# Cross attention of layer 1: context turned between the two key halves of a chunk, and transfers of weights and key pairs issued in other stages' programs

## Chip, core and metric

One core of a Trainium2 chip runs one program in one launch. Its engines are TensorE (PE), VectorE (DVE), ScalarE (ACT), GpSimd (POOL) and SyncE (SP); SP only issues transfers. The metric is the device time of that program in microseconds (us), lower is better.

## What is computed

Two layers act on `x`, 2 batches of 256 tokens by 256, with a context of 2 by 4096 rows of 192 numbers. Each layer is a cross attention into the context, a mixing stage and an expert mixture. The change concerns layer 1's cross attention and the borders to its neighbours:

```python
x = x + cross(layernorm(x), ctx)          # layer 1, 16 heads of 16
# in cross:
Qp = query @ Wq + bq
K = l2norm(ctx @ Wk + bk)                 # norm over all 256 columns of a row
V = ctx @ Wv + bv
Q = l2norm(Qp)
attn = softmax(Q @ K.T * SCALE)           # per head, 256 queries x 4096 keys
out = (attn @ V) @ Wo + bo + Qp
return layernorm(out) * gamma + beta
```

Before it stands layer 0's expert mixture, behind it layer 1's self attention (weights `w_q, w_k, w_v, w_o`), then layer 1's expert mixture.

## The kernel before

The program is a chain of blocks (`nc.Block()`). In a block each engine has its own instruction list, ordered by semaphores; at its end all five engines meet, so **a block lasts as long as its longest list**, SP's list of transfer issues too. A transfer's issue takes an engine's time, while its bytes travel on their own; a block does not wait for bytes unless an instruction in it does.

`l1_cross_attention` runs these blocks in order:

1. `l1x_weights`: `start_loads` issues 14 transfers, half on SP and half on ACT (line 1258); `finish_loads` is a block in which SP waits for all of them; then ACT and DVE split Wk and Wv into a high and a low part, `s.wkv` (L2181, L2188).
2. `l1x_queries`: layernorm of `x` (L131 to L158), the product with Wq, query norms, turned queries.
3. For each batch `l1x_keys_values`: 8 chunks of 512 context rows. A chunk's rows are turned by PE into PSUM banks 0 and 1 (`turn`, L541); ACT copies them to `cA_hi` and `cB` (L2313, L2314) and DVE makes the low parts (L2353, L2355). PE projects the two key halves d = 0 and 1 into banks 2 and 3 (L2265); ACT keeps their high part (L2320, two instructions for a half) and DVE the low part (L2364), ACT squares them (L2326), POOL adds the squares, PE sums them (L2283), DVE keeps the sums (L2380). PE projects values into banks 4 and 5 (L2275) and DVE keeps these (L2372). Chunk c+1 is turned while chunk c is projected. Chunks 2 to 5 are in a hardware loop on PE and DVE, 0 to 5 on ACT; the rest is written out.
4. For each batch `l1x_attention`: 128 steps of scores (L2470), exponential (ACT, L2455) and weighting (L2482). Keys come from `k_pairs`, a buffer of two halves. A half (16 steps) is filled by 12 transfers out of `keys` (`load_key_pairs`, L2418). There are 8 fillings for a batch; fillings 0 and 1 are issued at the end of `l1x_keys_values`, when the keys of chunks 0 to 3 and of 4 to 7 are there, and the others in the attention, each when its half has been used.
5. `fetch_l1_self_attention` (6 transfers) and `fetch_l1_mixture` (6 transfers) are blocks that only issue; then comes `l1x_output`: output product, bias, layernorm, sum into `x`.

The order in a chunk before is written out by hand:

```python
# PE:  project_keys(c) (both halves); turn(c + 1); sum_squares(c - 1); project_values(c)
# ACT: keys_hi(c, 0); keys_hi(c, 1); context_hi(c + 1); squares(c, 0); squares(c, 1)
# DVE: keys_lo(c, 0); keys_lo(c, 1); context_lo(c + 1); keep_norms(c - 1); keep_values(c)
```

Of the kernel before, what the change touches and what calls it, by code (L numbers as in the profile page):

```python
# [22 lines left out]
P = 128  # L23
# [1734 lines left out]
def l0_mixture(core, s):  # L1758
# [4 lines left out]
    with ExitStack() as ctx:  # L1763
# [11 lines left out]
        with ExitStack() as late:  # L1775
# [13 lines left out]
            with nc.Block() as block:  # L1789
                @block.tensor  # L1790
# [93 lines left out]
def fetch_l1_mixture(core, ctx):  # L1884

    s = Tiles()
    s.w_gu = core.sbuf(ctx, "w_gate_up1", [P, 2, 2, DC, M1])
    s.wd = core.sbuf(ctx, "w_down1", [P, 2, MT, D])
    s.arrived = [core.sem(ctx, f"moe1_w_arrived{i}", lasting=True) for i in range(2)]
    routed, _ = routed_weights(core)  # L1890
    with core.nc.Block() as block:
        @block.sync
        def _(sp):
            for e in range(2):
                fetch_expert(s, sp, e, routed, e)
    return s
# [178 lines left out]
def l1x_queries(core, s):  # L2075
# [3 lines left out]
    with ExitStack() as ctx:  # L2079
        xnT = core.sbuf(ctx, "xnT_l1x", [P, DC, T])  # L2080
        wq, bq = s.wq, s.bq
# [17 lines left out]
        with nc.Block() as block:  # L2099
            @block.tensor  # L2100
# [56 lines left out]
def l1x_weights(core, s):  # L2157

    nc, a = core.nc, core.args
    with ExitStack() as ctx:  # L2160
        raw = core.sbuf(ctx, "wkv1_raw", [P, 2, 2, D])
        hi = core.sem(ctx, "wkv1_hi")
        pairs = []
        for i, n in enumerate("kv"):
            w = a[f"L1_xattn_W{n}"]
            pairs += [(raw[:, 0, i, :], w[0:P, :]), (raw[0:CB, 1, i, :], w[P:CD, :]), (raw[CB:P, 1, i, :], w[P:CD, :])]
        finish_loads(core, start_loads(core, ctx, pairs + [
            (s.wq[:, :, :], a["L1_xattn_Wq"].rearrange("(c p) n -> p c n", p=P)),
            (s.bq[:, :], broadcast_rows(a["L1_xattn_bq"], P)),
            (s.bk[:, :], columns(a["L1_xattn_bk"])),  # L2170
            (s.bv[:, :], broadcast_rows(a["L1_xattn_bv"], P)),
            (s.bo[:, :], broadcast_rows(a["L1_xattn_bo"], P)),
            (s.gamma[:, :], broadcast_rows(a["L1_xattn_ln_gamma"], P)),
            (s.beta[:, :], broadcast_rows(a["L1_xattn_ln_beta"], P)),
            (s.wo[:, :, :], a["L1_xattn_Wo"].rearrange("(c p) n -> p c n", p=P)),
        ], "l1w"))
        with nc.Block() as block:
            @block.scalar
            def _(act):
                for c in range(2):  # L2180
# [11 lines left out]
def l1x_keys_values(core, b, s, keys, values, inv_norm, k_ready):  # L2192
# [5 lines left out]
    with ExitStack() as ctx:  # L2198
# [22 lines left out]
        with nc.Block() as block:  # L2221
# [12 lines left out]
            def _(sp):  # L2234
# [6 lines left out]
                for half in range(2):  # L2241
                    if b == 0:
                        sp.wait_ge(pairs_padded, half + 1)
                    sp.wait_ge(k_hi, (half + 1) * CHUNKS * 2)
                    sp.wait_ge(k_lo, (half + 1) * CHUNKS * 2 + 4)
                    load_key_pairs(sp, s, keys, 0, half, k_ready)

            @block.tensor
            def _(pe):
# [8 lines left out]
                def project_keys(c, slot):  # L2258
                    pe.wait_ge(c_hi, c * 2 + 4)
                    pe.wait_ge(c_lo, c * 2 + 4)  # L2260
                    for d in range(2):
                        pe.wait_ge(k_lo, c * 4 + 2 * d + 2)
                        pe.wait_ge(squared, c * 2 + d + 1)
                        for n, (part, operand) in enumerate(passes):
                            last = pe.matmul(psum[:, 2 + d, :], s.wkv[:, part, d * P:(d + 1) * P], operand[:, slot, :],  # L2265
                                             start=n == 0, stop=n == len(passes) - 1)
                        last.then_inc(k_done, 1)
# [701 lines left out]
```

## Time and profile before

| | us |
|---|---|
| median of 3 runs | 2123.61 |
| lowest, highest | 2123.42, 2126.72 |
| the profiled execution | 2128.06 |
| its span, first to last instruction | 2126.4 |
| mean granted TensorE clock | 0.942 of full |

The profiled execution lies 4.45 us above the median of the runs, and its span 1.66 us below its own time. Times in the rows are us from the span's start. In a timeline row stand the start, the busy time of the merged instructions, the engine (SPq and ACTq are their transfer issues, PEq is PE's sequencer), the line, the output and inputs with their sizes, the count, and in brackets the idle time of that engine just before with what ended it.

### The profile page before, as it was taken

How to read it: one execution, taken by the hardware profiler on the slowest of the kernel's cores; microseconds unless marked ns; L12 is line 12 of the kernel's file. 1: busy time of each engine (PE TensorE's matmuls, PEld its weight loads, DVE VectorE, ACT ScalarE, POOL GpSimd, SP SyncE). 2: the span in 40 equal slices, each digit the busy share in tenths (PEclk: the TensorE clock that was granted, in tenths of full speed). 3: DMA queues.
4: the chain of work that ended last, by engine and by line, in shares of the span. 5: the costliest groups of instructions: out<-in, count | busy, mean ns of one | idle time of the engine just before them, and what ended most of it. 6: DMA issues, size and time to landing. Idle time of an engine off the chain costs nothing. (4 is left out here: it accounts for less than half of the span.)

```text
span 2126.4 us, 33376 instructions
## 1 busy us (share of the span) xinstructions
PE 1898.8 (89%) x13464; PEld 1274.8 (60%) x13464; DVE 1096.3 (52%) x1550; ACT 1029.4 (48%) x1363; POOL 649.9 (31%) x315
## 2 busy tenths in 40 slices
PE   6899999999899999999999666948898899666999
PEld 2576766666566676766666344438444744343887
DVE  2577676675766758676550444238001700273665
ACT  1254454444544445444441322026897699524443
POOL 1026564554545646555473030011000100010000
PEclk9899999999999999999999786969999999877999
DMA  5410000001200000000030100023553446300221
GB/s 189 134 43 6 6 16 1 16 6 42 59 1 16 6 16 6 6 11 6 1 79 1 59 1 1 0 63 84 85 91 70 92 68 103 98 1 2 90 90 40
DMA packets 89923, 90.59 MB, mean 43 GB/s; under 512 B 29928, under 2 KB 79824, under 8 KB 86448
## 3 DMA queue, kind: packets, MB, share of 16 engines
q1 hardware_dynamic: 86912, 86.01, 16.7%
q10 hardware_dynamic: 2864, 2.51, 0.4%
q8 instruction: 107, 1.75, 0.4%
q14 instruction: 40, 0.33, 0.0%
HBM read 58.57 MB, written 8.91 MB: 32 GB/s over the span
## 5 line engine op out<-in xcount | busy, mean ns | idle before, releaser
L760 POOL TENSOR_TENSOR sums<-sums,probs 128x1024 f32<-128x1024 f32 x224 | 534.6, 2386 | 355.0 <-ACT probs L793 305.2
L844 DVE TENSOR_REDUCE part_max<-psum_banks 128x2 f32<-128x1024 f32 (+1 forms) x256 | 312.7, 1224 | 125.8 <-PE psum_banks L1006 121.3
L793 ACT ACTIVATE probs<-psum_banks 128x1024 f32<-128x1024 f32 x240 | 245.8, 1024 | 123.3 <-PE psum_banks L1052 116.1
L1066 PE MATMUL psum_banks<-probs,values 128*64 128x256 f32 x2048 | 278.4, 393 | 0.3 <-ACT probs L796 0.3
L771 ACT ACTIVATE keys<-psum_banks 64x512 fp32r<-64x512 f32 x256 | 151.6, 592 | 239.7 <-PE psum_banks L979 236.6
L2455 ACT ACTIVATE probs<-psum_banks,k_inv_norm 128x1024 f32<-128x1024 f32 x256 | 258.0, 1257 | 2.2 <-PE psum_banks L2470 2.2
L837 DVE TENSOR_TENSOR keys<-psum_banks,keys 64x512 fp32r<-64x512 f32 x256 | 176.2, 688 | 117.8 <-ACT keys L771 111.6
L1034 PE MATMUL psum_banks<-q_hi,keys 128*128 128x256 f32 x1024 | 184.6, 302 | 0.0
L1066 PEld LDWEIGHTS psum_banks<-probs,values 128*64 128x64 f32 x2048 | 124.4, 136 | 99.8 <-issue 60.1
L1034 PEld LDWEIGHTS psum_banks<-q_hi,keys 128*128 128x128 f32 x1024 | 138.0, 189 | 76.7 <-issue 51.7
L776 ACT ACTIVATE values<-psum_banks 128x512 f32<-128x512 f32 x128 | 76.5, 598 | 192.8 <-PE psum_banks L991 192.8
L2482 PE MATMUL psum_banks<-probs,values 128*32 128x256 f32 x2048 | 166.1, 397 | 2.3 <-ACT probs L2455 2.3
L2470 PEld LDWEIGHTS psum_banks<-q_parts_turned,k_pairs 64*128 64x128 f32 x1024 | 78.2, 190 | 116.3 <-ACT probs L2455 97.1
L2445 DVE COPY o_raw<-psum_banks 128x256 f32<-128x256 f32 x8 | 3.4, 424 | 270.3 <-PE psum_banks L2482 270.3
L2470 PE MATMUL psum_banks<-q_parts_turned,k_pairs 64*128 64x256 f32 x1024 | 130.6, 335 | 10.8 <-PEq L2221 10.8
L1042 PE MATMUL psum_banks<-shift,ones_r 64*128 64x512 f32 x512 | 128.8, 497 | 0.0
L991 PE MATMUL psum_banks<-wv_quad,cA_hi 128*128 128x256 f32 x512 | 109.9, 296 | 0.0
L1006 PE MATMUL psum_banks<-keys,q_hi 64*128 64x512 f32 x512 | 105.1, 404 | 0.5 <-DVE part_max L844 0.3
L979 PE MATMUL psum_banks<-cA_hi,wk_pair 128*128 128x512 f32 x256 | 87.5, 423 | 20.3 <-ACT values L776 10.5
L1052 PEld LDWEIGHTS psum_banks<-q_lo,keys 64*128 64x128 f32 x1024 | 97.6, 186 | 11.0
L1052 PE MATMUL psum_banks<-q_lo,keys 64*128 64x256 f32 x1024 | 102.9, 277 | 0.0
L991 PE MATMUL psum_banks<-wv_quad,cB 128*128 128x256 f32 x512 | 101.9, 280 | 0.0
(443 smaller groups left out, 3044.9 us busy)
## 6 DMA issues: line engine op xcount, KB each, us to landing
k_pairs<-keys SPq DMA_DIRECT2D x192, 128.0 KB, 4.3
ctx_tok<-in_ctx SPq DMA_DIRECT2D x16, 384.0 KB, 3.4
wk_pair<-wkv_parts SPq DMA_DIRECT2D x16, 256.0 KB, 2.9
wv_quad<-wkv_parts SPq DMA_DIRECT2D x8, 512.0 KB, 3.7
w_gate_up<-in_L_ffn_gate_proj_w SPq DMA_DIRECT2D x8, 512.0 KB, 4.0
w_gate_up<-in_L_ffn_up_proj_w SPq DMA_DIRECT2D x8, 512.0 KB, 4.9
w_down<-in_L_ffn_down_proj_w SPq DMA_DIRECT2D x8, 512.0 KB, 5.9
ctx_tok_b<-in_ctx SPq DMA_DIRECT2D x8, 384.0 KB, 4.7
```

Source lines behind the costliest of these rows:

```text
L760: pool.tensor_tensor(sums[:, :, :, :], probs[:, 0, :, :, :] if step == 1 else sums[:, :, :, :], probs[:, step % SLOTS, :, :, :], ALU.add). ...
L771: act.activation(keys[rows(h), m % 2, h, columns_of(c)], psum[rows(h), bank, :], ACT.Copy).then_inc(k_hi, 1)
L793: act.activation(probs[:, step % SLOTS, :, :, :], scores, ACT.Exp, scale=SCALE0).then_inc(p_ready, 1)
L837: dve.tensor_tensor(keys[rows(1 - h), m % 2, h, columns_of(c)], psum[rows(h), bank, :], keys[rows(h), m % 2, h, columns_of(c)].bitcast(F32 ...
L844: dve.tensor_reduce(part_max[:, :, i, c], psum[:, bank:bank + 2, 0:width], AX, ALU.max).then_inc(m_read, 1)
L991: last = pe.matmul(psum[:, bank, j * QW:(j + 1) * QW], operand[:, tile], wv_q[:, part, :], start=k == 0, stop=k == len(PASSES) - 1)
L1034: pe.matmul(psum[:, bank + h, j * L:(j + 1) * L], keys[:, m % 2, h, kt * P:(kt + 1) * P], q_hi[:, m % Q_SLOTS, h, :], start=j == 0, stop=F ...
L1052: last = pe.matmul(psum[:, bank + h, j * L:(j + 1) * L], keys[rows(h), m % 2, h, kt * P:(kt + 1) * P], q_lo[rows(h), m % 2, :], start=Fals ...
L1066: last = pe.matmul(psum[rows(h), 3, 0:L], values[:, kt, at:at + HD0], probs[:, step % SLOTS, h, j, :], start=kt == 0, stop=kt == KT - 1, t ...
L2455: act.activation(probs[:, step % 4, :, :], psum[:, bank:bank + 2, :].rearrange("p t (a q) -> p (t a) q", q=L), ACT.Exp, scale=inv_norm[:, ...
L2470: last = pe.matmul(psum[:, 2 + 2 * (step % 3) + h, pair * L:(pair + 1) * L], s.k_pairs[rows, half, pair, at:at + P], s.q_parts[rows, 2 * g ...
L2482: last = pe.matmul(psum[32 * r:32 * r + 32, g % 2, 0:L], s.values_flat[:, at:at + 32], probs[:, step % 4, r % 2 * 2 + r // 2, :], start=kt ...
```

## The change

Four things are changed. The three weights that are needed first (`Wk`, `Wv`, `Wq` with `bq`) get fixed places in memory from 144 KiB up, and their 8 transfers are issued by SP in layer 0's mixture block. `l1x_weights` issues the other 6 on SP while ACT and DVE split. In a chunk the context of c+1 is turned, copied and split between key half 0 and key half 1. Filling 1 of the key pairs is issued at the start of the attention. The 12 transfers of self attention and mixture are issued in the program of `l1x_output`.

```diff
+L1_WEIGHTS_AT = 144 * 1024
+def l1x_first_weights(core, ctx):
+    a, s = core.args, Tiles()
+    fixed = lambda name, shape, at: core.nc.alloc_sbuf_tensor_at(core.unused(name), shape, F32, offset=L1_WEIGHTS_AT + at)
+    s.raw = fixed("wkv1_raw", [P, 2, 2, D], 0)
+    s.wq = fixed("wq1", [P, DC, D], 16 * D)
+    s.bq = fixed("bq1", [P, D], 24 * D)
+    s.arrived = core.sem(ctx, "l1w_first_arrived", lasting=True)
...
-def l0_mixture(core, s):
+def l0_mixture(core, s, w_l1):
...
+                @block.sync
+                def _(sp):
+                    for dst, src in w_l1.pairs:
+                        sp.dma_start(dst, src).then_inc(w_l1.arrived, 16)
...
-def fetch_l1_mixture(core, ctx):
+def l1_mixture_weights(core, ctx):
...
-    routed, _ = routed_weights(core)
-    with core.nc.Block() as block:
-        @block.sync
-        def _(sp):
-            for e in range(2):
-                fetch_expert(s, sp, e, routed, e)
...
-def l1x_queries(core, s):
+def l1x_queries(core, s, first):
...
+            @block.sync
+            def _(sp):
+                sp.wait_ge(s.arrived, 16 * len(s.pairs))
...
-def l1x_weights(core, s):
+def l1x_weights(core, s, first):
...
-        finish_loads(core, start_loads(core, ctx, pairs + [
...
         with nc.Block() as block:
+            @block.sync
+            def _(sp):
+                with nc.allow_non_contiguous_dma(reason="vectors of a few hundred elements as columns"):
+                    for dst, src in s.pairs:
+                        sp.dma_start(dst, src).then_inc(s.arrived, 16)
+
             @block.scalar
             def _(act):
+                act.wait_ge(first.arrived, 16 * len(first.pairs))
```

In `l1x_keys_values`, SP's list, then PE's, ACT's and DVE's `chunk`:

```diff
-                for half in range(2):
-                    if b == 0:
-                        sp.wait_ge(pairs_padded, half + 1)
-                    sp.wait_ge(k_hi, (half + 1) * CHUNKS * 2)
-                    sp.wait_ge(k_lo, (half + 1) * CHUNKS * 2 + 4)
-                    load_key_pairs(sp, s, keys, 0, half, k_ready)
+                if b == 0:
+                    sp.wait_ge(pairs_padded, 2)
+                sp.wait_ge(k_hi, CHUNKS * 2)
+                sp.wait_ge(k_lo, CHUNKS * 2 + 4)
+                load_key_pairs(sp, s, keys, 0, 0, k_ready)
...
-                    project_keys(c, slot)
+                    project_keys(c, slot, 0)
                     if after:
                         turn(c + 1, *after)
+                    project_keys(c, slot, 1)
                     if not first:
                         sum_squares(c - 1, 1 - slot)
...
-                    for d in range(2):
-                        keys_hi(c, d)
+                    keys_hi(c, 0)
                     if more:
                         context_hi(c + 1, 1 - slot)
+                    keys_hi(c, 1)
...
-                    for d in range(2):
-                        keys_lo(c, d)
+                    keys_lo(c, 0)
                     if more:
                         context_lo(c + 1, 1 - slot)
+                    keys_lo(c, 1)
```

In `l1x_attention`, `l1x_output` and `l1_cross_attention`:

```diff
-                for n in range(2, HALVES):
-                    sp.wait_ge(pv_done, (n - 1) * HT)
+                for n in range(1, HALVES):
+                    if n >= 2:
+                        sp.wait_ge(pv_done, (n - 1) * HT)
                     load_key_pairs(sp, s, keys, n // 2, n % 2, k_ready)
...
-def l1x_output(core, s):
+def l1x_output(core, s, w_self, w_mixture):
...
+            @block.sync
+            def _(sp):
+                for dst, src in w_self.pairs:
+                    sp.dma_start(dst, src).then_inc(w_self.arrived, 16)
+                routed, _ = routed_weights(core)
+                for e in range(2):
+                    fetch_expert(w_mixture, sp, e, routed, e)
...
-def l1_cross_attention(core, ctx):
+def l1_cross_attention(core, ctx, first):
...
-    later = fetch_l1_self_attention(core, ctx), fetch_l1_mixture(core, ctx)
-    l1x_output(core, s)
+    later = l1_self_attention_weights(core, ctx), l1_mixture_weights(core, ctx)
+    l1x_output(core, s, *later)
```

The waits of a key half stay with it: PE projects half d of chunk c only when DVE has kept half d of chunk c-1 and ACT has squared it, and before half 0 it waits for the context of its chunk.

PE's list in chunk 6, the first that is written out behind the loop. Before, from key half 0 to the summed squares:

```order
L2265 MATMUL psum_banks<-c1A_hi,wkv 128x512 x2
L2265 MATMUL psum_banks<-c1A_lo,wkv 128x512
L2265 MATMUL psum_banks<-c1B,wkv 128x512 x2
L2265 MATMUL psum_banks<-c1A_hi,wkv 128x512 x2
L2265 MATMUL psum_banks<-c1A_lo,wkv 128x512
L2265 MATMUL psum_banks<-c1B,wkv 128x512 x2
L541 MATMUL psum_banks<-ident,ctx_tok 128x128 x8
L2283 MATMUL psum_banks<-ones,k_squared 128x1 x4
```

The same place of the changed kernel:

```order
L2280 MATMUL psum_banks<-c1A_hi,wkv 128x512 x2
L2280 MATMUL psum_banks<-c1A_lo,wkv 128x512
L2280 MATMUL psum_banks<-c1B,wkv 128x512 x2
L541 MATMUL psum_banks<-ident,ctx_tok 128x128 x8
L2280 MATMUL psum_banks<-c1A_hi,wkv 128x512 x2
L2280 MATMUL psum_banks<-c1A_lo,wkv 128x512
L2280 MATMUL psum_banks<-c1B,wkv 128x512 x2
L2298 MATMUL psum_banks<-ones,k_squared 128x1 x4
```

The eight transposes of the next chunk (L541) have moved ahead of the five products of key half 1; ACT's and DVE's context instructions move in the same way in their lists.

SP's list from the end of batch 0's token loads on, before (L2221 ends the keys' block, L2434 the attention's):

```order
L2236 COMPARE_AND_BRANCH
L2418 DMA k_pairs<-keys 16x2048 x24
L2221 UNCONDITIONAL_BRANCH
L2435 UNCONDITIONAL_BRANCH
L2418 DMA k_pairs<-keys 16x2048 x72
```

And in the changed kernel (L2237 ends the keys' block):

```order
L2252 COMPARE_AND_BRANCH
L2434 DMA k_pairs<-keys 16x2048 x12
L2237 UNCONDITIONAL_BRANCH
L2451 UNCONDITIONAL_BRANCH
L2434 DMA k_pairs<-keys 16x2048 x84
```

Twelve of the issues have moved from the keys' block to the attention's.

## Rows read from the trace of the kernel before

**Rows 1.** The page, busy time, share of the span and instructions of PE.

```profile
PE 1898.8 (89%) x13464; PEld 1274.8 (60%) x13464; DVE 1096.3 (52%) x1550; ACT 1029.4 (48%) x1363; POOL 649.9 (31%) x315
```

**Rows 2.** Timeline, from `start_loads` to the layernorm of the cross attention.

```profile
1382.87 0.93 SPq L1258 DMA_DIRECT2D wkv_raw<-in_L_xattn_Wk  x2
...
1386.13 0.43 SPq L1258 DMA_DIRECT2D beta<-in_L_xattn_ln_beta  x1
...
1394.00 1.29 DVE L2188 TENSOR_TENSOR wkv<-wkv_raw,wkv 128x512 fp32r<-128x512 f32 x2 [11.85 <-ACT wkv L2181]
...
1395.63 1.41 DVE L133 BATCH_NORM_STATS2 l1x_ln_stats<-x_stream 128x6 f32<-128x256 f32 x4
```

**Rows 3.** Waits of SP's queue, 1360 us to the end: total, times, longest.

```profile
SPq L1277 <- DMA wo<-in_L_xattn_Wo: 5.7, 1, 5.7
```

**Rows 4.** Timeline of batch 0's chunks: starts of 0, 1, then 5 with parts, 6, 7.

```profile
1428.13 1.19 PE L2265 MATMUL psum_banks<-c1A_hi,wkv 128*128 128x512 f32 x2 [2.67 <-issue]
...
1436.92 0.70 PE L2265 MATMUL psum_banks<-c1A_hi,wkv 128*128 128x512 f32 x2 [0.83 <-DVE c1B L2355]
...
1466.06 0.72 PE L2265 MATMUL psum_banks<-c1A_hi,wkv 128*128 128x512 f32 x2 [0.60 <-DVE c1B L2355]
...
1467.62 2.81 ACT L2320 ACTIVATE keys<-psum_banks,bk 64x512 f32 x4 [2.08 <-PE psum_banks L2265]
...
1468.49 3.10 DVE L2364 SCALAR_TENSOR_TENSOR keys<-psum_banks,bk,keys 64x512 f32 x4 [1.12 <-ACT keys L2320]
...
1471.56 1.27 ACT L2326 ACTIVATE k_squared<-psum_banks,bk 128x512 f32<-128x512 f32 x2
...
1472.34 0.69 DVE L2355 TENSOR_TENSOR c1B<-psum_banks,c1B 64x512 fp32r<-64x512 f32 x1
...
1473.13 0.71 PE L2265 MATMUL psum_banks<-c1A_hi,wkv 128*128 128x512 f32 x2 [0.38 <-issue]
1473.26 1.42 DVE L2372 TENSOR_TENSOR values<-psum_banks,bv 128x256 f32 x4
...
1480.06 0.70 PE L2265 MATMUL psum_banks<-c1A_hi,wkv 128*128 128x512 f32 x2 [0.23 <-issue]
```

**Rows 5.** Timeline, end of the keys' block and start of the attention, both batches.

```profile
1485.73 7.82 SPq L2418 DMA_DIRECT2D k_pairs<-keys  x12
...
1489.25 0.35 DVE L2403 RECIPROCAL k_inv_norm<-k_norm 128x32 f32<-128x32 f32 x1
1494.24 1.65 PE L2470 MATMUL psum_banks<-q_parts_turned,k_pairs 64*128 64x256 f32 x12 [5.70 <-PEq L2221]
...
1497.68 0.79 PE L2470 MATMUL psum_banks<-q_parts_turned,k_pairs 64*128 64x256 f32 x4
...
1499.42 0.79 PE L2470 MATMUL psum_banks<-q_parts_turned,k_pairs 64*128 64x256 f32 x4
...
1500.26 1.11 ACT L2455 ACTIVATE probs<-psum_banks,k_inv_norm 128x1024 f32<-128x1024 f32 x1 [0.62 <-PE psum_banks L2470]
...
1501.69 39.32 ACT L2455 ACTIVATE probs<-psum_banks,k_inv_norm 128x1024 f32<-128x1024 f32 x39 [0.32 <-PE psum_banks L2470]
...
1697.44 0.35 DVE L2403 RECIPROCAL k_inv_norm<-k_norm 128x32 f32<-128x32 f32 x1
1701.83 1.65 PE L2470 MATMUL psum_banks<-q_parts_turned,k_pairs 64*128 64x256 f32 x12 [5.10 <-PEq L2221]
```

**Rows 6.** Windows of 1 us; the clock stands behind POOL's part, before DMA.

```profile
1490.00:1491.00 1.00, 0.00 (x0) 0.00 (x0) 0.00 (x0) 0.00 (x0) 0.00 (x0) 0.94 1.21 205
```

**Rows 7.** The page, transfers: KB each, median us from issue to landing.

```profile
k_pairs<-keys SPq DMA_DIRECT2D x192, 128.0 KB, 4.3
```

**Rows 8.** Timeline, end of the attention of batch 1 to the self attention.

```profile
1834.06 0.42 DVE L2445 COPY o_raw<-psum_banks 128x256 f32<-128x256 f32 x1 [31.25 <-PE psum_banks L2482]
...
1840.27 3.64 PE L2525 MATMUL psum_banks<-ident,o_raw 128*128 128x128 f32 x16 [6.28 <-PEq L1891]
...
1858.85 3.65 PE L1229 MATMUL psum_banks<-ident,self_raw 128*128 128x128 f32 x16 [8.12 <-PEq L65]
```

More of the change, by code:

```diff
@@ L1755, in fetch_l0_mixture @@
     return s
-def l0_mixture(core, s):
+L1_WEIGHTS_AT = 144 * 1024
[6 more added lines that the diff above has]
+    s.arrived = core.sem(ctx, "l1w_first_arrived", lasting=True)
+    s.pairs = []
+    for i, n in enumerate("kv"):
+        w = a[f"L1_xattn_W{n}"]
+        s.pairs += [(s.raw[:, 0, i, :], w[0:P, :]), (s.raw[0:CB, 1, i, :], w[P:CD, :]), (s.raw[CB:P, 1, i, :], w[P:CD, :])]
+    s.pairs += [(s.wq[:, :, :], a["L1_xattn_Wq"].rearrange("(c p) n -> p c n", p=P)),
+                (s.bq[:, :], broadcast_rows(a["L1_xattn_bq"], P))]
+    return s
+def l0_mixture(core, s, w_l1):
     nc, psum, a = core.nc, core.psum, core.args
@@ L2256, in turn, with project_keys @@
                     turn_tokens(pe, core, 0, tok[:, slot, :, :]).then_inc(turned, 1)
-                def project_keys(c, slot):
-                    pe.wait_ge(c_hi, c * 2 + 4)
-                    pe.wait_ge(c_lo, c * 2 + 4)
-                    for d in range(2):
[L2262 to L2267, printed above, removed]
+                def project_keys(c, slot, d):
+                    if d == 0:
+                        pe.wait_ge(c_hi, c * 2 + 4)
+                        pe.wait_ge(c_lo, c * 2 + 4)
+                    pe.wait_ge(k_lo, c * 4 + 2 * d + 2)
+                    pe.wait_ge(squared, c * 2 + d + 1)
+                    for n, (part, operand) in enumerate(passes):
+                        last = pe.matmul(psum[:, 2 + d, :], s.wkv[:, part, d * P:(d + 1) * P], operand[:, slot, :],
+                                         start=n == 0, stop=n == len(passes) - 1)
+                    last.then_inc(k_done, 1)
                 def project_values(c, slot):
@@ L2593, in l1_cross_attention @@
     s.o_raw = core.sbuf(ctx, "o_raw1", [P, GROUPS, T])
-    with ExitStack() as early:
-        s.wq = core.sbuf(early, "wq1", [P, DC, D])
-        s.bq = core.sbuf(early, "bq1", [P, D])
-        l1x_weights(core, s)
-        l1x_queries(core, s)
+    a = core.args
+    s.arrived = core.sem(ctx, "l1w_arrived", lasting=True)
+    s.pairs = [(s.bk[:, :], columns(a["L1_xattn_bk"])),
+               (s.bv[:, :], broadcast_rows(a["L1_xattn_bv"], P)),
+               (s.bo[:, :], broadcast_rows(a["L1_xattn_bo"], P)),
+               (s.gamma[:, :], broadcast_rows(a["L1_xattn_ln_gamma"], P)),
+               (s.beta[:, :], broadcast_rows(a["L1_xattn_ln_beta"], P)),
+               (s.wo[:, :, :], a["L1_xattn_Wo"].rearrange("(c p) n -> p c n", p=P))]
+    l1x_weights(core, s, first)
+    l1x_queries(core, s, first)
     with ExitStack() as big:
@@ L2622, in fetch_l1_self_attention @@
     s.raw = core.sbuf(ctx, "self_raw", [P, 4, DC, D])
-    s.loads = start_loads(core, ctx,
-                          [(s.raw[:, i, :, :], a[f"L1_attn_w_{n}"].rearrange("(c p) n -> p c n", p=P))
-                           for i, n in enumerate("qkvo")]
-                          + [(s.cos[:, :, :], a["rope_cos"].rearrange("(t p) d -> p t d", p=P)),
-                             (s.sin[:, :, :], a["rope_sin"].rearrange("(t p) d -> p t d", p=P))], "self")
+    s.arrived = core.sem(ctx, "self_w_arrived", lasting=True)
+    s.pairs = [(s.raw[:, i, :, :], a[f"L1_attn_w_{n}"].rearrange("(c p) n -> p c n", p=P)) for i, n in enumerate("qkvo")]
+    s.pairs += [(s.cos[:, :, :], a["rope_cos"].rearrange("(t p) d -> p t d", p=P)),
+                (s.sin[:, :, :], a["rope_sin"].rearrange("(t p) d -> p t d", p=P))]
+    s.loads = [(s.arrived, 16 * len(s.pairs))]
     return s
```

27 lines of the change are left out of this document (7 added, 20 removed).

## The prediction

> **What bounds the kernel now.** The page comes first: PE is busy for 89% of the span [rows 1]. That is an average over stages, and none of it says what the borders between blocks cost. The chain of work that ended last is no help either: it reaches back through the last mixture and covers 7% of the span. So I read the timeline at each place that the diff touches, and asked at each border which engine's list ended last.
>
> Four stretches stand out in which PE waits for something other than arithmetic. (a) Between `start_loads` and the layernorm, from 1382.87 to 1395.63, nothing is computed but the split of the weights, and SP sat 5.7 us on the landing of `wo`, which is needed only at the very end of the attention [rows 2, 3]. (b) In a chunk of the keys' block PE waits 0.60 us for DVE's low part of the next context, and DVE before that 1.12 us for ACT's first key part [rows 4]. (c) The keys' block of batch 0 has its last arithmetic at 1489.60 (DVE's reciprocal), but SP issues until 1485.73 + 7.82 = 1493.55, and PE starts its scores at 1494.24, 5.70 us idle [rows 5]. (d) The attention of batch 1 ends on DVE at 1834.48 and the output's transposes start at 1840.27, after two blocks that only issue [rows 8].
>
> **(a) Weights: 8.9 us.** The 8 first transfers go into layer 0's mixture block, where SP had nothing to do, and land tens of us before they are used: cost nothing; without that cover they would cost 8 issues. The wait for the landing is gone. What is left is one block: ACT and DVE split (DVE's part is 1.29 us [rows 2] and ACT's first half stands ahead of it: some 2 us in all), and SP issues 6 transfers. Before, SP issued 7 from 1382.87 to 1386.56, 0.53 us each [rows 2]; six take 3.2, so SP's list is now the longest, to 1386.05. From SP's last issue to the next block's first instruction it is 1494.24 - 1493.55 = 0.69 us [rows 5]. The layernorm then starts at 1386.7 instead of 1395.63: 8.9 us. Bounds: 8.0 if an issue costs the 0.65 us of the key pairs (7.82 / 12 [rows 5]), 10.2 if SP's list were hidden and DVE's end (1384.9, and 0.5 of border) decided. The six land within some 7 us of their issue, and `l1x_queries`, where SP now waits for them, starts 5 us later and computes for far longer: hidden. The 0.53 us holds with all issues on SP; before, ACT took half of them beside it.
>
> **(b) Order in a chunk: 8.6 us.** I walk through one chunk with the durations of chunk 5, time 0 being PE's first key product [rows 4]. ACT's first key part starts at 1.56 (1467.62 - 1466.06) and DVE's at 2.43. Before, all four key parts stood ahead of the context on both engines: DVE 2.43 + 3.10, then 1.41 for the context (1471.62 to 1473.03), PE's next chunk right behind: 7.07 to 7.30 us. Now two key parts do: ACT's context is over at 1.56 + 1.40 + 1.13 = 4.1 (1.13 being 1470.43 to 1471.56), DVE's at 4.15 + 1.41 = 5.6. PE needs one thing more for the next half 0: the square of this chunk's half 0, which ACT makes after key half 1, at 4.1 + 1.40 + 0.64 = 6.15, and some 0.1 to 0.35 for the wait itself: 6.3 to 6.5. DVE's own work is 3.10 + 1.41 + 0.23 + 1.42 = 6.2. PE's is its period less its idle time, 7.07 - 0.38 = 6.69; as the ends of its matmuls are modelled and overlap, I take 6.6. So **PE becomes the bound of a chunk**, with ACT's square and DVE close behind. Key half 1 of the next chunk is not held up: it comes 2.1 us after half 0 and needs DVE's part of 7.15 and ACT's square of 7.85, against 8.7.
>
> Six intervals from chunk 1 to chunk 7 take 1480.06 - 1436.92 = 43.1 us; six of 6.6 take 39.6: 3.5. The first interval, 1436.92 - 1428.13 = 8.8 at low clock, loses PE's wait of 0.83 and a little more by the earlier turn: 1.0. The last chunk has no turn and is unchanged, but DVE comes to it 0.2 later. Per batch 4.3, for both 8.6. Bounds: 2.4 for both if loop instructions hold a chunk at 7.1; 10.8 if PE can do 6.4.
>
> **(c) Filling 1 of the key pairs: 8.0 us.** SP's 12 issues leave the keys' block; its list then ends long before the arithmetic. The block ends with DVE: 1489.60, and from DVE's end at 1395.29 to the next block it was 0.34 us [rows 2]. Scores start at 1489.95 instead of 1494.24: 4.3. In batch 1, 1697.79 + 0.34 = 1698.1 instead of 1701.83: 3.7. What hides the twelve now: filling 1 is used from step 16. Issues take 7.8 us and the last lands 4.3 later [rows 7], 12.1 us after the block's start; the steps take 1.01 us (39.32 / 39) and the first ones 1.74 [rows 5], so step 16's scores come at about 16. Four us of room. Behind them in SP's queue stands filling 2, which waits for step 16's weighting anyway. Without cover a late landing would cost what it is late. Bounds 6 and 8.6.
>
> **(d) Weights of the later stages: 5.5 us.** Both issue blocks go; transposes start at 1834.48 + 0.34 = 1834.8 instead of 1840.27. The 12 issues, all on SP, take 6.4 us of a block that lasts 18 (1840.27 to 1858.85 [rows 8]), and the self weights, issued first, land before its end. Bounds 5.0 and 6.7, by the clock (below).
>
> Sum: 8.9 + 8.6 + 8.0 + 5.5 = **31.0 us**. Against the profiled execution's 2128.06 that is 2097.1, its span 2095.4. The median of the runs shown is 4.45 lower, and as the removed stretches are the same in any run, I forecast 2123.61 - 31.0 = **2092.6**.
>
> **The clock at the new borders.** In the microsecond from 1490 the granted clock averaged 0.94, so it fell from 2.4 to 1.2 GHz near its end, after PE had last worked at 1488.5 [rows 5, 6]. The first steps then ran at 1.74 us and ACT idled 0.62 + 0.32 us [rows 5]. The changed kernel starts the scores at 1489.95, before that fall. I count nothing for it: the quiet tail of the keys' block is unchanged.
>
> The Trainium skill, "TensorE: Matmul & The Clock Gate", section "What's actually happening", has throttled as the default state that activity releases and idleness restores. By that rule the shorter gaps could leave the clock up; the trace agrees that it fell after idle time, and no run here shows what a gap of 1.4 us does.
>
> **Rivals.**
>
> *The order in the chunk gives little (11%).* The register instructions of the loops stand in the stretches that are now critical; the loop's 7.30 against 7.07 behind it speaks for some of that. At 7.1 a chunk, (b) is 2.4: 2098.8; at no gain 2101.2. Against it: PE's and DVE's pure loads are 6.6 and 6.2.
>
> *The clock stays up over the shorter borders (9%).* Then the attentions gain 0.94 each, and the output's 16 transposes, 3.64 us at low clock [rows 8], up to 1.2: 2089.5.
>
> *Transfers not hidden (4%).* Filling 1 lands late because twelve issues beside the start of the attention go slower than 0.65 us. Each us beyond the room of four costs one, twice; at double issue time 2 x 3.8: 2100.2.
>
> *A border doesn't shorten (4%).* Another engine's list, or the border itself, takes the place of SP's: with (c) at half, 2096.6, with (a) at half 2097.
>
> *Slower (3%).* The attention starts sooner behind the quiet tail, and the clock, down, does not come back. A step costs 1.74 instead of 1.01 us, 0.73 more; the 31.0 us are used up at 42 of 256 steps, and with a whole batch at low clock (128 steps) the time is 2186. For it: the clock does fall here. Against it: in batch 0 it came back within about six steps [rows 5], and PE is as dense then as before.
>
> **How the numbers follow.** The forecast as summed, give or take 4 us for its small terms, has 69%. From below, the clock's gain and a PE at 6.4 set 2087; from above, the rivals of order and landing set 2101. Outside lie some 12%. A measurement of this kernel tells about 0.2% (4.2 us) from no change; all but the slow rival and a failure of several terms are beyond it: faster 96%, same 1.5%, slower 2.5%.
>
> **What would show it.** From `start_loads`' place to the layernorm some 4 us instead of 12.8. PE's chunk starts 6.6 us apart, with idle times before them of 0.1 to 0.3. No PEq wait above 2 us before the first scores, and no wait for a transfer at step 16. SP's twelve issues beside `l1x_output`. I would be wrong by most if chunk starts stay 7 us apart, if PE waits for the key pairs, or if the clock stays at 1.2 GHz behind a border.

## The result and the profile after

| us | before | changed |
|---|---|---|
| median of 4 runs | 2124.66 | 2086.75 |
| lowest, highest | 2123.42, 2126.72 | 2085.78, 2087.84 |
| profiled execution | 2128.06 | 2086.96 |
| its span | 2126.4 | 2085.3 |
| mean granted clock | 0.942 | 0.950 |

The ratio is 0.9821, with a 95% interval of 0.9804 to 0.9838. The medians differ by 37.9 us; in a second measurement on another occasion (e9, below) by 38.0. The forecast was 31.0 us, its time 2092.6 and its low end 2087.0: the direction was right and each of the four waits shrank as described, but the time lies below the range, by 0.25 us, and the gain is 6.9 us larger than the sum. (The time is only 5.85 us off, because a fourth run has moved the median before from 2123.61 to 2124.66.)

The spans of the two profiled executions differ by 41.1 us, 3.2 of them ahead of every changed instruction: layer 0's mixture ends at 1382.16 before and at 1378.98 after, and 2.85 of that lead are there by 107 us. It is variation between executions (the end of layer 0 lay between 1376.7 and 1382.4 in the profiles of this study, whatever was changed behind it). From the same ACT instruction at 107 us on, layer 0 took 1274.42 us before, 1274.09 in the changed kernel and 1274.18 in e3 (below), so the transfers issued in it cost it nothing. So I count from its end: 744.24 us were left to the end of the span, now 706.32, which is 37.92 less and agrees with the medians. Cut at starts and ends from the timelines:

| stretch | before | changed | less | forecast |
|---|---|---|---|---|
| (a) layer 0's end to the layernorm | 13.47 | 3.97 | 9.50 | 8.9 |
| layernorm to chunk 0 of batch 0 | 32.50 | 32.28 | 0.22 | 0 |
| (b) chunk 0 to DVE's last instruction, batch 0 | 61.47 | 55.92 | 5.55 | 4.3 |
| (b) the same, batch 1 | 61.89 | 56.42 | 5.47 | 4.3 |
| (c) DVE's last instruction to the scores, batch 0 | 4.64 | 0.30 | 4.34 | 4.3 |
| (c) the same, batch 1 | 4.04 | 0.31 | 3.73 | 3.7 |
| attentions of batch 0 and 1 | 265.05 | 263.97 | 1.08 | 0 |
| (d) end of the attention to the output's transposes | 5.79 | 0.32 | 5.47 | 5.5 |
| (d) the transposes to the self attention | 18.58 | 16.76 | 1.82 | 0 |
| self attention to the end | 267.55 | 266.80 | 0.75 | 0 |

The timeline of the changed kernel at the weights, to be compared with [rows 2]:

```profile
1379.68 0.38 SPq L2191 DMA_DIRECT2D bk<-in_L_xattn_bk  x1
...
1380.38 1.29 DVE L2204 TENSOR_TENSOR wkv<-wkv_raw,wkv 128x512 fp32r<-128x512 f32 x2 [1.41 <-ACT wkv L2197]
...
1382.04 0.43 SPq L2191 DMA_DIRECT2D wo<-in_L_xattn_Wo  x1
...
1382.95 1.41 DVE L133 BATCH_NORM_STATS2 l1x_ln_stats<-x_stream 128x6 f32<-128x256 f32 x4
```

SP's list is the longest, as forecast, but its six issues take 2.79 us, 0.47 each, and the border behind the last 0.48.

A chunk of batch 0 from its first key product to the next chunk's (ACT's rows are from the same timeline), against [rows 4]:

```profile
1423.03 0.70 PE L2280 MATMUL psum_banks<-c1A_hi,wkv 128*128 128x512 f32 x2
...
1424.27 1.04 PE L541 MATMUL psum_banks<-ident,ctx_tok 128*128 128x128 f32 x8
...
1425.06 0.71 PE L2280 MATMUL psum_banks<-c1A_hi,wkv 128*128 128x512 f32 x2
...
1428.51 0.69 ACT L2342 ACTIVATE k_squared<-psum_banks,bk 128x512 f32<-128x512 f32 x1
...
1429.29 0.40 PE L2290 MATMUL psum_banks<-wkv,c1B 128*128 128x256 f32 x2
1429.52 0.63 PE L2280 MATMUL psum_banks<-c1A_hi,wkv 128*128 128x512 f32 x2
```

No row of PE has a bracket: nothing is waited for. The six intervals from chunk 1 to chunk 7 as windows, first before and then changed. After the length stand busy time and count of PE, PEld, DVE, ACT and POOL, then the granted clock, the DMA share and GB/s.

```profile
1436.92:1480.06 43.14, 40.14 (x277) 36.01 (x277) 35.61 (x66) 30.53 (x48) 7.72 (x7) 1.00 0.42 87
```

```profile
1423.03:1461.62 38.59, 38.59 (x276) 35.69 (x277) 35.71 (x66) 31.24 (x48) 7.70 (x6) 1.00 0.46 97
```

PE is busy all the time, 38.59 / 6 = 6.43 us a chunk. Before, its busy time alone read 40.14 / 6 = 6.69 for the same work.

The end of the keys' block and the start of the attention in batch 0, against [rows 5]:

```profile
1470.80 0.35 DVE L2419 RECIPROCAL k_inv_norm<-k_norm 128x32 f32<-128x32 f32 x1
1471.40 20.86 SPq L2434 DMA_DIRECT2D k_pairs<-keys  x14
...
1471.45 1.65 PE L2487 MATMUL psum_banks<-q_parts_turned,k_pairs 64*128 64x256 f32 x12 [1.37 <-PEq L2237]
```

And the output, against [rows 8]:

```profile
1801.00 0.42 DVE L2462 COPY o_raw<-psum_banks 128x256 f32<-128x256 f32 x1 [31.26 <-PE psum_banks L2499]
1801.69 0.39 SPq L2533 DMA_DIRECT2D self_raw<-in_L_attn_w_q  x1
...
1801.74 1.94 PE L2550 MATMUL psum_banks<-ident,o_raw 128*128 128x128 f32 x16 [0.81 <-PEq L2450]
...
1806.87 3.72 PE L2560 MATMUL psum_banks<-wo,o1T 128*128 128x256 f32 x16 [1.38 <-DVE o1T L2574]
```

The sixteen transposes take 1.94 us where they took 3.64: PE stood idle for 0.81 us ahead of them instead of 6.28. Windows of 1 us over that place, before and then changed:

```profile
1835.00:1836.00 1.00, 0.00 (x0) 0.00 (x0) 0.00 (x0) 0.00 (x0) 0.00 (x0) 0.82 0.19 25
1836.00:1837.00 1.00, 0.00 (x0) 0.00 (x0) 0.00 (x0) 0.00 (x0) 0.00 (x0) 0.50 0.97 316
...
1840.00:1841.00 1.00, 0.73 (x4) 0.76 (x5) 0.00 (x0) 0.59 (x1) 0.77 (x2) 0.50 1.03 371
```

```profile
1801.00:1802.00 1.00, 0.26 (x3) 0.29 (x4) 0.42 (x1) 0.12 (x1) 0.30 (x2) 1.00 0.00 0
1802.00:1803.00 1.00, 1.00 (x12) 1.00 (x11) 0.56 (x2) 1.00 (x1) 1.00 (x1) 1.00 0.23 32
```

The clock fell to 1.2 GHz before; now it stays at 2.4.

### The profile page after: what moved, and what is told of

Same layout as the page of the kernel before. It is cut to its first block and busy times, and to the rows that moved or that the text cites. A ratio compares the mean times of both kernels' runs of the same rounds, so it can differ in the third digit from the quotient of the medians.

```text
span 2085.3 us, 33327 instructions
## 1 busy us (share of the span) xinstructions
PE 1888.4 (91%) x13464; PEld 1269.3 (61%) x13464; DVE 1096.4 (53%) x1550; ACT 1031.0 (49%) x1363; POOL 650.1 (31%) x315
```

## Experiments

### Each part alone

Four kernels carry one part of the change each, with the code shown ahead. Their cores:

```diff
# e1: order in a chunk (PE's list; ACT's and DVE's in the same way)
-                    project_keys(c, slot)
+                    project_keys(c, slot, 0)
                     if after:
                         turn(c + 1, *after)
+                    project_keys(c, slot, 1)
# e2: filling 1 in the attention
-                for n in range(2, HALVES):
+                for n in range(1, HALVES):
# e3: first weights in layer 0, six transfers beside the split
-            l0_mixture(core, w_mixture)
+            w_l1 = l1x_first_weights(core, layer)
+            l0_mixture(core, w_mixture, w_l1)
# e4: twelve issues in the output's program
-    later = fetch_l1_self_attention(core, ctx), fetch_l1_mixture(core, ctx)
-    l1x_output(core, s)
+    later = l1_self_attention_weights(core, ctx), l1_mixture_weights(core, ctx)
+    l1x_output(core, s, *later)
```

**e1, the order.** 

> The kernel before with the new order in a chunk and nothing else. Trace of the changed kernel: chunk starts 6.42 us apart, six intervals and the first one gain 5.5 us in batch 0 and about as much in batch 1. Theory 'PE is the bound of a chunk at 6.42, less than the 6.6 I took': 10.9 us faster, chunk starts 6.42 apart, no idle time of PE ahead of them, everything else as before. Rival 'part of the gain of the changed kernel's chunks came with the other parts' (SP's list without filling 1, fixed places of weights): less than 9 us, starts 6.6 or more apart.

**e2, the filling.** 

> The kernel before with filling 1 of the key pairs issued in the attention and nothing else. Theory: the end of the keys' block moves to DVE's last instruction plus 0.3 us, 4.3 us in batch 0 and 3.7 in batch 1, and the scores at the start of the attention run at low clock for some tenths of a us less: 8.0 to 9.0 us faster. Rival 'the transfers are not hidden in part': 6 to 7.5, with a wait of PE for key pairs at step 16.

**e3, the weights.** 

> The kernel before with the first weights issued in layer 0's mixture and the other six beside their splitting, and nothing else. Theory: 9.5 us between the end of layer 0 and the layernorm, 0.2 behind it: 9.7 faster. Rival 'the 3.2 us by which the two profiled executions differ ahead of the first changed instruction belong to this part' (places in memory, a longer program in layer 0): 12 to 13 us faster. If it is 9.7, those 3.2 us are variation between executions, which arises in the first 110 us.

**e4, the output.** 

> The kernel before with the twelve issues in the output's program and nothing else. Theory 'the clock stays up over the shorter border': transposes at 1.9 us instead of 3.64, self attention's first transposes 7.3 us earlier counted from the end of the attention, 8.1 us faster in all with 0.8 in the self attention. Rival 'only the two blocks of issues count' (the working of the prediction): 5.5 us faster, transposes still 3.6 us.

| | median | ratio to before, 95% | less in the stretches it touches | in the changed kernel |
|---|---|---|---|---|
| before, same chip | 2125.73 | | | |
| e1 order | 2117.26 | 0.9959, 0.9940 to 0.9978 | 5.81 + 5.30 = 11.1 | 11.0 |
| e2 filling | 2119.18 | 0.9967, 0.9954 to 0.9980 | 4.34 + 3.72 = 8.1 | 8.1 |
| e3 weights | 2117.57 | 0.9964, 0.9951 to 0.9978 | 9.5 | 9.5 |
| e4 output | 2118.89 | 0.9967, 0.9954 to 0.9979 | 5.47 + 1.76 = 7.2 | 7.3 |

The runs scatter by 5 to 10 us here (the kernel before by 14.6), so the medians can't tell 8 from 11; the stretches can. Each part gives alone what it gives in the changed kernel, within 0.1 us: in these stretches the four don't act on each other, and 35.9 of the 37.9 us are theirs. Each figure rests on one profile of each kernel, though, and a stretch that a kernel leaves alone also varies: (a) took 13.02 to 13.47 us in the five profiles that have it as before (before, e1, e2, e4, e5). The wholes add up to less than the stretches, 30.0 us by the medians and 33.7 by the profiles counted from layer 0's end, because code that the part leaves alone took longer in some of them. In e1 chunks start 6.42 to 6.51 us apart with no other part present, so neither SP's shorter list nor the places of the weights has to do with it. In e3 layer 0 ends at 1379.14, among the others, and its stretch gives 9.5: the 3.2 us ahead of the change aren't this part's. In e2 the attentions are no shorter (132.47 and 133.02), so their 1.1 us in the changed kernel aren't the filling's; nor does any part alone shorten what follows the output. In e1 that stretch was even 3.1 us longer, 270.62. That is taken up below.

### The clock at the output's border

```diff
# e5, on the kernel before: PE's list in the two blocks that only issue
+            @block.tensor
+            def _(pe):
+                for n in range(13):      # 26 in the second block
+                    pe.transpose(core.psum[:, 7, n % 4 * P:(n % 4 + 1) * P], core.ident[:, :], core.ident[:, :])
```

> The kernel before, in whose two blocks that only issue (between the attention of batch 1 and the output) PE also turns the identity into an unused bank, 13 times and 26 times, some 0.12 us each at full clock, so that it works while the others issue. Its outputs are unused. Theory 'the clock at the output border follows PE's idle time': the border stays 5.8 us, but the granted clock stays 1.00 over it and the 16 transposes behind it take 1.9 us instead of 3.64; from their start to the self attention's first transposes 16.8 us instead of 18.6. Rival 'the faster output of the changed kernel comes from the transfers that no longer run beside its start (the DMA engines were busy at 308 to 383 GB/s there)': 3.6 us and 18.6 stay, since the same transfers still run beside it.

The profile of e5, windows and then the timeline:

```profile
1830.00:1831.00 1.00, 1.00 (x11) 0.93 (x9) 0.00 (x0) 0.00 (x0) 0.00 (x0) 1.00 0.16 44
...
1834.00:1835.00 1.00, 0.54 (x5) 0.30 (x3) 0.00 (x0) 0.00 (x0) 0.00 (x0) 1.00 1.13 266
1835.00:1836.00 1.00, 0.23 (x2) 0.26 (x3) 0.00 (x0) 0.09 (x1) 0.27 (x2) 1.00 0.99 365
```

```profile
1833.97 1.35 SPq L1887 DMA_DIRECT2D w_down<-in_L_ffn_down_proj_w  x1
...
1835.77 1.94 PE L2536 MATMUL psum_banks<-ident,o_raw 128*128 128x128 f32 x16 [1.23 <-PEq L1897]
```

With PE at work over the border the clock stays at 2.4 GHz, and the transposes take 1.94 us with the transfers running beside them at up to 387 GB/s. From them to the self attention it is 17.00 us instead of 18.58. So 1.6 of the 1.8 us are the clock's, and the rival, DMA traffic, explains at most the 0.2 that are left. In this profile one SP issue took 1.35 us, which made the border 6.54 us. The median is that of before (2127.29 to 2127.43, ratio 1.0002, 0.9990 to 1.0013); 1.6 us are too little for it to show. The Trainium skill, "TensorE: Matmul & The Clock Gate", section "What's actually happening", has activity release the throttle and idleness bring it back; by that rule this is what useless work on PE should do, and the trace agrees, 1.94 against 3.64 us.

### How much room filling 1 has

```diff
# e6, on the changed kernel, SP's list of the attention
-                    if n >= 2:
-                        sp.wait_ge(pv_done, (n - 1) * HT)
+                    sp.wait_ge(pv_done, (n - 1) * HT if n >= 2 else (2, 8)[b])
```

> The changed kernel, with filling 1 of the key pairs begun later: behind the weighting of step 2 in batch 0 and of step 8 in batch 1. In the changed kernel the twelve issues last to 7.8 us behind the first score, the last transfer lands 4.3 later, and by its rows the scores of step 16 come 18.5 us behind the first score, so the room is 6.7 us and not the 4 that I took. Batch 0: issues begin 5.2 us later, room is left, nothing lost. Batch 1: issues begin 11.5 us later, so PE waits some 5 us for a transfer at step 16 and the attention lasts 137 us instead of 132. Rival 'the room is the 4 us of the prediction': batch 0 loses about 1.2 and batch 1 about 7.5. Rival 'transfers beside the attention take much longer than their median': both lose more.

PE's waits in e6, over the attention of batch 0 and then over that of batch 1 (total, times, longest):

```profile
PE psum_banks L2486 <- DMA k_pairs<-keys: 0.7, 1, 0.7
...
PE psum_banks L2486 <- DMA k_pairs<-keys: 6.3, 1, 6.3
```

The kernel's median is 2098.20; from layer 0's end on it took 716.70 us, where the changed kernel took 706.32. My expectation had miscounted: the first score row holds three steps, not two, so in the changed kernel step 16's scores come 1477.94 + 11 x 1.005 = 1489.0, 17.5 us behind the first and not 18.5. In batch 0 the issues began 5.35 us later and 0.7 us of it showed: a room of 4.6 us, close to the 4 of the prediction. In batch 1 it was 12.97 less 6.25, 6.7 us. Of this, 1.3 come from its first steps, which ran longer at low clock than in the changed kernel: step 7's scores start 9.78 us behind the first ones instead of 8.49, ahead of any late transfer. From the first issue to the end of PE's wait it was 13.0 and 12.2 us, the 7.8 + 4.3 of [rows 5, 7]. A late filling costs more than its wait: behind the 6.25 us of waiting the clock had fallen, and steps of 1.74, 1.74 and 1.32 us follow, 1.8 us more than at full clock. With the 1.3 us of the first steps that makes the 9.3 by which batch 1's attention is longer (141.3 us instead of 132.0). So the changed kernel is inside its room, by four to five steps, and the price of leaving it is 1.8 us above the wait.

### What bounds a chunk now, and what bounds it next

```diff
# e7, on the changed kernel: batch 0 with 4 of 5 products for the values, batch 1 with 3
-                            for n, (part, operand) in enumerate(passes):
+                            kept = passes[:4 - b]
+                            for n, (part, operand) in enumerate(kept):
```

> The changed kernel with less work for PE in a chunk: values are projected with four of the five products in batch 0 and with three in batch 1 (the low rows of the values are left out), 0.47 and 0.94 us less of 6.42 at 0.117 us each. Theory 'PE is the bound, and ACT's square of key half 0 stands close behind': the square is over 6.17 us after a chunk's start, so chunk starts are 6.25 to 6.35 us apart in both batches, with a small idle time of PE released by ACT. Rival 'PE stays the bound': 5.95 in batch 0 and 5.48 in batch 1. Rival 'PE is not the bound': 6.42 in both.

The timeline of e7 in batch 0, PE's chunk starts and all of DVE between two of them:

```profile
1442.73 1.53 DVE L2381 SCALAR_TENSOR_TENSOR keys<-psum_banks,bk,keys 64x512 f32 x2
...
1443.44 0.73 PE L2280 MATMUL psum_banks<-c1A_hi,wkv 128*128 128x512 f32 x2
...
1444.30 0.16 DVE L2397 COPY k_inv_norm<-psum_banks 128x4 f32 x1
1444.49 1.42 DVE L2389 TENSOR_TENSOR values<-psum_banks,bv 128x256 f32 x4
1445.94 1.53 DVE L2381 SCALAR_TENSOR_TENSOR keys<-psum_banks,bk,keys 64x512 f32 x2
1447.54 0.69 DVE L2370 TENSOR_TENSOR c1A_lo<-psum_banks,c1A_hi 128x512 fp32r<-128x512 f32 x1
1448.26 0.69 DVE L2372 TENSOR_TENSOR c1B<-psum_banks,c1B 64x512 fp32r<-64x512 f32 x1
1448.98 1.53 DVE L2381 SCALAR_TENSOR_TENSOR keys<-psum_banks,bk,keys 64x512 f32 x2
...
1449.69 0.73 PE L2280 MATMUL psum_banks<-c1A_hi,wkv 128*128 128x512 f32 x2
```

The interval falls to 6.25 us in both batches (1443.44 to 1449.69; in batch 1 1628.70 to 1634.95; all from chunk 1 on are 6.23 to 6.35), although PE has 0.47 less in the one and 0.94 less in the other. So PE was the bound at 6.42, and something else is at 6.25. It isn't ACT's square by its own weight, as I had it: DVE's rows stand one behind the other without a gap, from 1442.73 to the same place at 1448.98, 6.25 us (the prediction had DVE's own work at 6.2). PE's wait does end with ACT's square, as in this row of batch 1, but ACT itself waits 0.91 us a chunk for DVE's key part:

```profile
1628.70 0.74 PE L2280 MATMUL psum_banks<-c1A_hi,wkv 128*128 128x512 f32 x2 [0.50 <-ACT k_squared L2343]
```

The kernel as a whole gained nothing (median 2088.06, 706.52 us from layer 0's end). The 1.0 us that the chunks of each batch gained was lost again: 0.3 us in each batch behind the last chunk's start, 0.8 in the attentions and 0.8 from the self attention on.

### Shorter still, and where it went

In the changed kernel PE waits for the first context rows at the start of each keys' block (5.12 us in batch 1). e8 loads chunks 0 and 1 a stage earlier, e9 is the changed kernel again.

```diff
# e8: in the queries' block for batch 0, in the attention of batch 0 for batch 1
+                start_tokens(sp, core, s, 0)
                 sp.wait_ge(s.arrived, 16 * len(s.pairs))
...
                     load_key_pairs(sp, s, keys, n // 2, n % 2, k_ready)
+                    if n == 1 and b + 1 < B:
+                        start_tokens(sp, core, s, b + 1)
...
-                with sp.Fori(0, CHUNKS // 2) as i:
+                with sp.Fori(1, CHUNKS // 2) as i:
```

> The changed kernel, and the context rows of chunks 0 and 1 are loaded in the stage before the keys' block: for batch 0 in the query block, for batch 1 in the attention of batch 0. Now PE waits at the start of each keys' block for them, 5.1 us in batch 1. Theory: PE's first turning starts 0.3 to 0.5 us behind the block's start instead of 4.5, 4.2 us each, 8.4 for both; and if the clock follows idle time, batch 1's first chunk, whose border is then short, runs at full clock (turn 1.0 instead of 1.97, chunk 0 to 1 about 7 instead of 8.3), 2 more: 8.5 to 11 us faster than the changed kernel. Rival 'something else ends last at the start of the block' (POOL's filling of values and of key pairs, 8 us in batch 0): batch 0 gains little, 4 to 6 in all. Rival 'no gain': the tokens land no earlier beside the key pairs' transfers.

> The changed kernel once more, for its distance to the kernel before and to the one with earlier tokens on the same chip. By the parts run alone, each by the stretches that it touches (order 11.0, filling 8.1, weights 9.5, output 7.2) it is 35.8 us faster than before; by the first comparison of medians 37.9. By the prediction's sum 31.0. If the parts add up, it is 34 to 38; if some of them give more together than alone, above 38.

e9 is 38.0 us faster than before (2087.85 to 2125.80, ratio 0.9825, 0.9812 to 0.9839), at the upper end of what I expected. e8 reaches 2086.35 (0.9813, 0.9800 to 0.9826): 1.5 us from e9, with overlapping runs, and not 8.5. Yet its edit did what it should: 4.17 us less ahead of chunk 0 of batch 0 and 4.91 of batch 1, and 0.6 in batch 1's first chunk. Behind it the same code took longer: batch 1's attention 132.92 instead of 131.98, transposes to self attention 18.36 instead of 16.76, and the rest, from the self attention to the end, 270.58 instead of 266.80, 6.3 us in all. Windows of e8 in the output:

```profile
1799.00:1800.00 1.00, 0.41 (x2) 0.17 (x2) 0.56 (x1) 0.00 (x0) 1.00 (x1) 1.00 0.89 264
1800.00:1801.00 1.00, 0.21 (x1) 0.21 (x2) 0.73 (x2) 0.00 (x0) 0.34 (x1) 0.77 0.96 244
1801.00:1802.00 1.00, 1.00 (x3) 0.82 (x4) 0.00 (x0) 0.00 (x0) 0.00 (x0) 0.50 0.86 129
```

The border ahead is as short as in the changed kernel (0.33 us), PE's rows up to here lie the same way to 0.01 us, and still the clock falls at the output product, which then takes 5.26 us instead of 3.72.

To see whether the edit or its place in time does that, three kernels shift everything behind the split of the weights with unused transfers on SP:

```diff
# e10, e11: on e8, 3 and 6 transfers; e12: on the changed kernel, 3
+    s.pairs += [(s.o_raw[:, i % 4, i // 4 * D:(i // 4 + 1) * D], broadcast_rows(a["L1_xattn_bo"], P)) for i in range(3)]
     l1x_weights(core, s, first)
```

> The kernel with earlier tokens, and three more transfers of bo (into parts of o_raw that nothing has written yet) issued in the block that splits the first weights: SP's list there is 3 x 0.47 = 1.4 us longer, and everything behind it starts 1.4 us later; nothing else changes. With earlier tokens the stretches that the edit touches gained 9.7 us, but the output lost 1.6 and the self attention and mixture 3.8, in code that is the same; the clock was low there in other places. Theory 'which level the clock has behind a gap depends on where in time the gap lies, not on the code': a shift of 1.4 us changes the output's 18.4 and the 270.6 from the self attention to the end by a us or more, and the whole differs from the unshifted kernel by something other than +1.4. Rival 'the loss is tied to the edit' (another layout, tokens' transfers): 18.4 and 270.6 stay, the whole is 1.4 longer.

> The same with six more transfers, 2.8 us later. Theory of position in time: the output and what stands behind it take another value again, or that of the changed kernel (16.8 and 266.8 to 267.2). Rival 'tied to the edit': 18.4 and 270.6, the whole 2.8 us longer than with earlier tokens alone.

> The changed kernel with the three more transfers, 1.4 us later from the query block on. Theory of position in time: somewhere behind it a stretch of unchanged code differs from 16.8 at the output or 266.8 to 267.2 behind it by a us or more. Rival 'the changed kernel's clock pattern is a property of its code': the same durations, 1.4 us longer in all (some 2089.2 by the median of 2087.85 of its second measurement).

| us | changed | e12 | e8 | e10 | e11 |
|---|---|---|---|---|---|
| median | 2087.85 (e9) | 2090.60 | 2086.35 | 2087.02 | 2085.97 |
| layer 0's end to the layernorm | 3.97 | 5.44 | 3.97 | 5.44 | 7.79 |
| layernorm to chunk 0 | 32.28 | 34.20 | 28.11 | 30.14 | 27.92 |
| transposes to self attention | 16.76 | 16.75 | 18.36 | 18.35 | 16.81 |
| self attention to the end | 266.80 | 267.19 | 270.58 | 270.59 | 268.33 |
| layer 0's end to the end | 706.32 | 710.11 | 703.37 | 706.97 | 703.08 |

e10 to e12 ran on another chip than e8 and e9; the kernel before took 2125.90 there and 2125.80 here. e11 spends 3.8 us more at the weights than e8 and is not slower: its output is back at the changed kernel's duration, and what follows is 2.3 us shorter than in e8, though 1.5 longer than in the changed kernel. So these two losses don't come with the edit alone. The third may be: batch 1's attention took 132.92, 132.92 and 133.04 us in e8, e10 and e11, against 131.98, 131.87 and 131.96 in the changed kernel, e9 and e12. A shift of 1.5 us left the output and what follows as they were, in e10 and in e12, within 0.02 us of e8 and e9: there the rival was right and the theory's forecast missed. But in both the stretch ahead of chunk 0 is longer, by 2.0 and 1.9 us. There the windows show the clock at work; the changed kernel, and then e12, over the same instructions:

```profile
1382.95:1415.23 32.28, 14.68 (x64) 12.46 (x65) 14.09 (x40) 7.50 (x18) 8.84 (x5) 0.66 0.22 58
```

```profile
1383.83:1418.03 34.20, 16.59 (x65) 14.08 (x65) 14.08 (x40) 7.50 (x18) 8.84 (x5) 0.60 0.27 61
```

DVE, ACT and POOL have the same busy time; PE has 1.91 us more at a mean clock of 0.60 instead of 0.66. It doesn't take a shift to get that. In e1 and e2 nothing is changed up to chunk 0, and the same stretch reads, e1 first and then e2:

```profile
1394.10:1425.20 31.10, 13.53 (x64) 11.15 (x65) 14.08 (x40) 7.50 (x18) 8.83 (x5) 0.72 0.17 43
```

```profile
1395.39:1428.99 33.60, 16.01 (x64) 13.58 (x65) 14.08 (x40) 7.50 (x18) 8.83 (x5) 0.60 0.15 39
```

Before, e4 and e5, unchanged up to there as well, took 32.50, 32.60 and 33.67 us. What is shown: the same code gets another clock from one profile to the next, worth up to 2.6 us in this stretch, and from the self attention to the end the same code took 266.8 to 270.6. That the place in time decides is argued from single profiles. Not shown is the rule by which the level is chosen. The Trainium skill, "TensorE: Matmul & The Clock Gate", section "What's actually happening", has the chip's judgement run freely, not restarted by the kernel, so that the place of a change of level depends on where the work falls; the trace agrees in that e11 and e8 differ. By that rule executions whose earlier part differs in length should also come out differently. Ahead of chunk 0 the trace agrees, in the 31.10 to 33.67 us of the five profiles just named. At the output it doesn't: in the profiles of the changed kernel, e6, e7, e9 and e12, whose layer 0 ends between 1378.39 and 1380.68, it took 16.76, 16.75, 16.75, 16.76 and 16.75 us. What fixes the place stays open.

## Why the prediction was right and where it fell short

**(a) Weights, 8.9 forecast, 9.5 measured.** The mechanism was right to the engine: SP's list ends last, the transfers in layer 0 cost nothing. The sizes were taken from dearer rows: an issue is 0.47 us there and not 0.53, the border 0.48 and not 0.69. As the stretch itself took 13.02 to 13.47 us where it is unchanged, the gain is 9.1 to 9.5.

**(b) Order in a chunk, 8.6 forecast, 11.0 measured.** This is the term that was mis-sized most. That PE becomes the bound was right, shown by e7 and by the windows. The step that failed is "I take 6.6": PE's own work is 6.42 us. The period less the idle time shown (6.69) is no pure load, since a matmul's modelled end lies past the place at which the next could start. The last pair of value products begins 0.23 us ahead of the next chunk when nothing is waited for (1429.29 to 1429.52). Before, in the timeline of PE, it stood here:

```profile
1472.36 0.40 PE L2275 MATMUL psum_banks<-wkv,c1B 128*128 128x256 f32 x2
```

The next chunk began at 1473.13 [rows 4], 0.77 us later, so 0.54 us were idle where the row says 0.38. After an idle time the first pair also runs 0.70 instead of 0.63. Both corrections lead from 7.07 to about 6.45. Six intervals then give 4.5 us a batch and not 3.5, 2.1 of the 2.4 us for both batches. The 0.2 us a batch by which DVE was to come later to the last chunk didn't show: from chunk 7's start to DVE's last instruction it is 9.53 us in both batches, and was 9.54 and 9.97. The walk's time for ACT's square, 6.15 us behind the chunk's start, was good (6.17). The first interval gave its 1.0 in batch 0 and only 0.5 in batch 1. The rival that loop instructions hold a chunk at 7.1 found nothing: chunks in the loop and behind it start 6.42 us apart.

**(c) Filling 1, 8.0 forecast, 8.1 measured.** Right in both batches, the 0.3 us of the border included. The room of four us was near the 4.6 that e6 shows in batch 0, in part by luck: step 16's scores come 17.5 us behind the first ones and not 16, and the last transfer ends PE's wait 13.0 us behind the first issue and not 12.1.

**(d) Weights of the later stages, 5.5 forecast, 7.3 measured.** The border gave 5.47. The other 1.8 is a second step that failed, the sum's missing term for the clock: it is the rival "the clock stays up over the shorter borders", which came true at the output and which I had counted at nothing in the sum. I had the transposes at up to 1.2 us of gain; they alone gave 1.7. At the attention's start the clock fell all the same, to 0.50 ahead of the first scores at 1471.45; PE had last worked at 1470.08:

```profile
1470.00:1471.00 1.00, 0.08 (x1) 0.00 (x0) 0.55 (x3) 0.23 (x1) 0.00 (x0) 0.82 0.00 0
1471.00:1472.00 1.00, 0.55 (x4) 0.58 (x6) 0.15 (x1) 0.59 (x1) 0.00 (x0) 0.50 0.00 0
```

The sentence of the prediction that the quiet tail is unchanged fits that, and I then carried its answer to the output, where PE works up to 0.81 us ahead of the transposes.

**Unchanged code, nothing forecast, 2.0 measured** (0.2 + 1.1 + 0.75). No part alone gave it: both attentions took 264.6 to 265.5 us in before and e1 to e5, and 263.7 to 264.0 in the changed kernel, e9 and e12 (264.75 in e7). The experiments show the clock moving unchanged stretches by as much or more. I take it for the same thing; that is argued, not shown.

Together: 31.0 + 0.6 + 2.4 + 0.1 + 1.8 + 2.0 = 37.9. All misses of the sum have one sign: where rows differed, the size was taken on the careful side. The low end of the range took in two of them, PE at 6.4 and the clock, and not the 0.6 of (a) and the 2.0 of unchanged code. The slower rival found nothing to speak for it: behind the keys' block the clock is back at 2.4 GHz within 7 us of its fall.

## What to carry to other kernels

Read an engine's pure load from start to start in a place where nothing is waited for, not as period less idle time: the ends of matmuls are modelled and hide part of a wait. When a border or wait of PE is shortened, price the clock behind it too, as a term of the sum, at both levels, with rows of the same instructions; and judge an edit by the stretches that it touches, because code behind it that hasn't changed can give or take some us by the clock it happens to get. Transfers that are needed late cost nothing in a program in which SP is idle, as long as the room is worked out from first issue to last landing: here 12.2 to 13.0 us for twelve.

## What the runs showed that was not expected

- The same PE rows, behind the same gap of 0.81 us, had the clock at 1.00 in one kernel and at 0.50 five us later in another (changed kernel and e8). A gap's length doesn't settle what comes.
- Nine us taken out of two waits (e8) moved the median by 1.5 us; 3.8 us put in on top of that (e11) moved it by -0.4.
- Useless transposes kept the clock up over a border of 6.5 us and saved 1.6 us behind it (e5).
- Up to chunk 0 of batch 0, five profiles of the same code took 31.10 to 33.67 us, at a mean granted clock of 0.72 to 0.60.
